# Keys, values and bias of the second attention: made in a stage of their own, or in the first stage and kept in DRAM

## The reference, cut to what matters

```
hd = DIM // HEADS            # 16
scale = hd ** (-0.5)
q = (x @ Wq).reshape(B, N, HEADS, hd)
k = (context @ Wk).reshape(B, M, HEADS, hd)
v = (context @ Wv).reshape(B, M, HEADS, hd)
scores = q k^T * scale, masked by context_mask; softmax over the 77 rows; times v; then @ Wo
```

## Time and profile before

| | us |
|---|---|
| median of 3 runs (lowest, highest) | 1813.8 (1812.35, 1814.16) |
| the profiled execution, its own time | 1812.47 |
| span of the profiled execution | 1810.7 |
| PE busy | 1554.4 (86%) |
| DVE busy | 1110.4 (61%) |
| ACT busy | 824.6 (46%) |
| POOL busy | 706.7 (39%) |

### The profile page before, as it was taken

The page is one execution under the profiler, slowest core; times in us unless marked ns, Lnnn a source line. Parts: engine busy times, 40 slices in busy tenths (PEclk is TensorE's granted clock), DMA queues, the critical chain, the costliest instruction groups (busy, mean ns, idle before and its releaser), DMA issues. The chain is left out here.

```text
span 1810.7 us, 39194 instructions
## 1 busy us (share of the span) xinstructions
PE 1554.4 (86%) x12604; PEld 1143.3 (63%) x12605; DVE 1110.4 (61%) x1945; ACT 824.6 (46%) x1516; POOL 706.7 (39%) x521
## 2 busy tenths in 40 slices
PE   4798798897977599999999994899978599999996
PEld 1433334234337478888888881777768478888885
DVE  4687787787868634444554441888868744444443
ACT  1563654645633355555554440566754322222221
POOL 2401303104000125555554431677760045556554
PEclk9899899898985799999999995799995799999998
DMA  4321311322228245555542222200006243333333
GB/s 134 111 71 47 123 62 46 116 69 97 67 89 279 90 148 139 139 139 139 136 116 46 45 34 52 70 25 24 25 1 233 86 134 61 58 58 59 60 59 44
DMA packets 104311, 159.85 MB, mean 88 GB/s; under 512 B 10810, under 2 KB 69998, under 8 KB 104110
## 3 DMA queue, kind: packets, MB, share of 16 engines
q1 hardware_dynamic: 73007, 117.52, 19.9%
q0 software_dynamic: 29952, 40.91, 12.9%
q10 hardware_dynamic: 1279, 0.46, 0.1%
HBM read 91.49 MB, written 67.37 MB: 88 GB/s over the span
## 5 line engine op out<-in xcount | busy, mean ns | idle before, releaser
L1243 PE MATMUL e_ph<-e_zTt,weights_a 128*128 128x256 f16 x3744 | 426.7, 275 | 29.9 <-issue 27.5
L1243 PEld LDWEIGHTS e_ph<-e_zTt,weights_a 128*128 x3744 | 361.6, 98 | 94.6 <-issue 50.4
L1376 DVE TENSOR_TENSOR e_hl<-e_h,e_hh 128x512 f16<-128x512 f32 x156 | 104.5, 690 | 230.7 <-ACT e_hh L1342 230.7
L1197 POOL DMA_INDIRECT e_zt<-token_parts,slot_token x156 | 163.4, 1048 | 210.6 <-issue 198.8
L1328 ACT ACTIVATE e_h<-e_ph,e_b 128x256 f32<-128x256 f32 x312 | 130.6, 470 | 234.9 <-PE e_ph L1243 157.5
L1207 POOL DMA_INDIRECT token_rows<-e_ysb,slot_token x78 | 148.2, 1900 | 208.9 <-DVE e_ysb L1393 194.7
L1257 PE MATMUL e_pyt<-weights_b,e_hh 128*128 x1248 | 210.7, 273 | 0.7 <-DVE e_ysb L1393 0.7
L640 ACT ACTIVATE probs<-lower_banks,shift 128x1024 f32<-128x1024 f32 x128 | 137.5, 1110 | 92.1 <-PE lower_banks L500 91.7
L1207 POOL DMA_INDIRECT out_dram<-e_ysb,slot_token x78 | 124.4, 1595 | 131.0 <-DVE e_ysb L1397 107.4
L1257 PE MATMUL e_pyt<-weights_b,e_hl 128*128 x624 | 170.1, 273 | 0.0
L1367 DVE SCALAR_TENSOR_TENSOR e_g<-e_ph,e_h 128x512 f32<-128x512 f32 x78 | 53.9, 691 | 173.8 <-PE e_ph L1243 173.8
(11 more groups left out here) (228 smaller groups left out, 2847.0 us busy)
## 6 DMA issues: line engine op xcount, KB each, us to landing
weight_parts<-w_split SPq DMA_DIRECT2D x32, 512.0 KB, 3.3
weights_a<-weight_parts SPq DMA_DIRECT2D x16, 1024.0 KB, 7.5
x_sb<-in_u SPq DMA_DIRECT2D x24, 512.0 KB, 5.1
weight_parts<-x_sb SPq DMA_DIRECT2D x24, 512.0 KB, 3.4
w_raw<-in_w1T SPq DMA_DIRECT2D x16, 512.0 KB, 4.4
w_raw<-in_w2T SPq DMA_DIRECT2D x16, 512.0 KB, 4.7
weights_b<-weight_parts SPq DMA_DIRECT2D x8, 1024.0 KB, 9.5
token_parts<-x_sb SPq DMA_DIRECT2D x8, 1024.0 KB, 5.3
```

Source lines behind the costliest of these rows:

```text
L1197: pool.indirect_dma_start(zt[:, i % 2, c, :], None, g.zrows, at).then_inc(ld[i % 2], 16)
L1243: last = pe.matmul(ph[:, q, f, :], up_w(wp, e, k, 2 * q + f), zTs[:, s, 2 * zp + k, :], start=(n == 0), stop=(n == 5))
L1376: dve.tensor_tensor(hl[:, s, 2 * q:2 * q + 2, :], src[:, q % 2], hh[:, s, 2 * q:2 * q + 2, :], ALU.subtract).then_inc(lo_done, 1)
```

## The change: what it does, and the diff

The first stage gets what the context stage did. ACT issues the loads of Wv, Wk and the mask behind its nine loads; PE makes the values and keys behind the eight `kv` products, in the banks of `tr`; ACT spreads the values behind its copy of `vctx`; DVE converts the mask behind `summarise` and makes the keys last; POOL's zeros and head masks stand behind its constants. The results `g.k1`, `g.v1`, `g.bias1` are stored to DRAM at the start of the first attention's SP stream, behind the three stores of zeros. `attention1_context` is gone. At the start of `attention1` ACT issues the loads of Wq, keys, bias, values and Wo, and waits stand where each is first used.

```diff
--- before
+++ after
@@ line 173 @@
             act.dma_start(gk[:], a["kn_g"].partition_broadcast(P)).then_inc(ld_g, 16)
+            for w, src in ((wv1, a["Wv1"]), (wk1, a["Wk1"])):
+                act.dma_start(w[:, 0, :], src[0:P, :]).then_inc(ld_second, 16)
+                act.dma_start(w[0:DC - P, 1, :], src[P:DC, :]).then_inc(ld_second, 16)
+            act.dma_start(mask8[:], a["mask1"].partition_broadcast(P)).then_inc(ld_second, 16)
@@ line 188 @@
             act.copy(g.vctx[:], kv[:, :, D:2 * D]).then_inc(sq_done, 1)
+            act.wait_ge(v1_mm, 1)
+            act.wait_ge(made, 1)
+            for b in range(B):
+                own_v = tr[0:M, b // 2, b % 2 * D:b % 2 * D + D].rearrange("p (h o d) -> p h o d", o=2, d=HD1)
+                for o in range(2):
+                    act.copy(g.v1[:, b, o:H1:2, o * HD1:(o + 1) * HD1], own_v[:, :, o, :]).then_inc(v1_ev, 1)
             act.wait_ge(v_step, 16)
@@ line 209 @@
             pool.wait_ge(g.consts, 4)
+            pool.memset(g.v1[:], 0.0).then_inc(made, 1)
+            pool.affine_select(out=own2[:], in_=g.ones[:, 0:8], compare_op=ALU.is_ge, fill=0.0, base=0,
+                               pattern=[[-HD1, 8]], channel_multiplier=1).then_inc(made, 1)
+            pool.wait_ge(made, 2)
+            pool.affine_select(out=own[:], in_=own2[:], compare_op=ALU.is_ge, fill=0.0, base=HD1 - 1,
+                               pattern=[[HD1, 8]], channel_multiplier=-1).then_inc(made, 1)
             pool.wait_ge(v_step, 9)
@@ line 248 @@
             summarise(dve, g, 1, 0, T, True)
+            dve.wait_ge(ld_second, 16 * 5)
+            dve.tensor_copy(mask1[:], mask8[:]).then_inc(k1_step, 1)
+            dve.wait_ge(made, 3)
+            dve.tensor_reduce(odd[:], own[:].rearrange("p (r o) -> p o r", o=2), AX.X, ALU.add).then_inc(k1_step, 1)
+            dve.wait_ge(k1_step, 2)
+            dve.tensor_scalar(g.bias1[:], mask1[:], 1.0, -MASKED, ALU.subtract, ALU.mult).then_inc(k1_step, 1)
             dve.wait_ge(p_step, 4)
@@ line 268 @@
             dve.tensor_tensor(khl[:, 1], kn[:], khl[:, 0], ALU.subtract).then_inc(v_step, 1)
+            dve.wait_ge(k1_mm, 1)
+            for hg in range(2):
+                dve.scalar_tensor_tensor(kT1[:, hg].rearrange("p b m -> p (b m)"), tr[:, 2 + hg, 0:B * M], SCALE1,
+                                         mask1[:].rearrange("p b m -> p (b m)"), ALU.mult, ALU.mult).then_inc(k1_step, 1)
+            dve.wait_ge(k1_step, 5)
+            for b in range(B):
+                for hg in range(2):
+                    dve.tensor_tensor(g.k1[:, b, hg], kT1[:, hg, b:b + 1, :].to_broadcast([P, 2, M]),
+                                      odd[:].rearrange("p (o n) -> p o n", n=1).to_broadcast([P, 2, M]),
+                                      ALU.mult).then_inc(k1_done, 1)
+            dve.wait_ge(k1_done, 2 * B)
             dve.wait_ge(v_step, 22)
@@ line 291 @@
             last.then_inc(kv_done, 1)
+
+            pe.wait_ge(ld_second, 16 * 5)
+            for b in range(B):
+                for k, r in ((0, P), (1, DC - P)):
+                    last = pe.matmul(tr[0:M, b // 2, b % 2 * D:b % 2 * D + D], g.ctxT[0:r, k, b, 0:M], wv1[0:r, k, :],
+                                     start=(k == 0), stop=(k == 1))
+            last.then_inc(v1_mm, 1)
+            for hg in range(2):
+                for k, r in ((0, P), (1, DC - P)):
+                    last = pe.matmul(tr[:, 2 + hg, 0:B * M], wk1[0:r, k, hg * P:(hg + 1) * P], g.ctxT[0:r, k, :, 0:M],
+                                     start=(k == 0), stop=(k == 1))
+            last.then_inc(k1_mm, 1)
+            pe.wait_ge(v1_ev, 2 * B)
             pe.wait_ge(hi_done, 1)
@@ line 393 @@
                          ).then_inc(g.cleared, 16)
+            for home, made in zip(g.second, (g.k1, g.v1, g.bias1)):
+                sp.dma_start(home, made[:]).then_inc(second_kept, 16)
             for i, gate in enumerate((a["routerT"], a["gate"])):
@@ line 422 @@
             sp.wait_ge(g.cleared, 48)
+            sp.wait_ge(second_kept, 48)
             for i in range(2):
@@ line 1430 @@
-def attention1_context(nc, g, a, at):
...
-def attention1(nc, g, at):
+def attention1(nc, g, a, at):
@@ line 1613 @@
                     t = base + c
+                    if c == 0:
+                        pe.wait_ge(ld_q, 16)
                     pe.wait_ge(zT_ev, t + 1)
@@ line 1648 @@
                 if live(d):
+                    if d == 0:
+                        pe.wait_ge(ld_o, 16)
                     pe.wait_ge(o_ev, base + d + 1)
@@ line 1657 @@
         def _(act):
+            act.dma_start(at.wq[:], a["Wq1"].rearrange("(k p) n -> p k n", p=P)).then_inc(ld_q, 16)
+            act.dma_start(at.k[:], g.second[0]).then_inc(ld_k, 16)
+            act.dma_start(at.bias[:], g.second[2]).then_inc(ld_k, 16)
+            act.dma_start(at.v[:], g.second[1]).then_inc(ld_v, 16)
+            act.dma_start(at.wo[:], a["Wo1"].rearrange("(k p) n -> p k n", p=P)).then_inc(ld_o, 16)
+
             def body(base, b0, c, live):
                         act.wait_ge(s_done, base + c)
+                    else:
+                        act.wait_ge(ld_k, 32)
                     act.copy(keys[:].rearrange("p (n h) o m -> p n h o m", n=1),
@@ line 1681 @@
                 if live(d + 1) and (d + 1) % TB == 0:
+                    if d + 1 == 0:
+                        act.wait_ge(ld_v, 16)
                     act.copy(v[:].rearrange("p (o h) d -> p o h d", o=1), at.v[:, bass.ds(b0 + (d + 1) // TB, 1)]
@@ line 1750 @@
                         dve.wait_ge(pt_done, 4 * (t - SLOT) + 4)
+                    if c == 1:
+                        dve.wait_ge(ld_k, 32)
                     dve.wait_ge(s_done, t + 1)
@@ line 1827 @@
+    g.second = [nc.dram_tensor(f"second_{n}", shape, F32, kind="Internal").ap()
+                for n, shape in (("k", [P, B, 2, 2, M]), ("v", [M, B, H1, 32]), ("bias", [P, B, M]))]
+
     def rows_of(w, k0, k):
@@ line 1840 @@
             m = Mem(nc, st)
+            g.k1 = m.sb("k1_made", [P, B, 2, 2, M])
+            g.v1 = m.sb("v1_made", [M, B, H1, 32])
+            g.bias1 = m.sb("bias1_made", [P, B, M])
             g.kctx = m.sb("kctx", [P, 2, 2 * B, MP], F16)
@@ line 1871 @@
             at.wo = m.sb("wo1", [P, 2, D])
-            attention1_context(nc, g, a, at)
-            attention1(nc, g, at)
+            attention1(nc, g, a, at)
```

More of the change, by code:

```diff
@@ L136, in attention0_inputs @@
         gabs = m.sb("gabs", [P, 1])
+        wk1 = m.sb("wk1", [P, 2, D])
+        wv1 = m.sb("wv1", [P, 2, D])
+        mask8 = m.sb("mask8", [P, B, M], U8)
+        mask1 = m.sb("mask1f", [P, B, M])
+        own = m.sb("own", [P, 8])
+        own2 = m.sb("own2", [P, 8])
+        odd = m.sb("odd", [P, 2])
+        kT1 = m.sb("kT1", [P, 2, B, M])
         kv = m.ps("kv_c", [M, B, 2 * D])
@@ L144, in attention0_inputs @@
         hi_done, kt_done, kt_ev = m.sem("c_hi"), m.sem("c_ktd"), m.sem("c_ktev")
+        ld_second, made, v1_mm, k1_mm = m.sem("k_ld"), m.sem("k_made"), m.sem("k_vmm"), m.sem("k_kmm")
+        v1_ev, k1_step, k1_done = m.sem("k_vev"), m.sem("k_step"), m.sem("k_bd")
         recycle(nc, g, m)
@@ L385, in attention0 @@
         w_hi, w_lo = m.sem("a_w_hi"), m.sem("a_w_lo")
+        second_kept = m.sem("a_second")
         recycle(nc, g, m)
@@ L1560, in attention1 @@
         ld = [m.sem(f"b_ld{i}") for i in range(2)]
+        ld_q, ld_k, ld_v, ld_o = (m.sem("b_ld_" + n) for n in "qkvo")
         recycle(nc, g, m)
```

74 lines of the change are left out of this document (removed).

## The result

| | changed kernel | kernel before, same chip |
|---|---|---|
| median (lowest, highest), us | 1791.0 (1786.71, 1792.0) | 1813.14 |
| ratio, 95% interval | 0.9874 [0.986, 0.9888] | |
| the profiled execution, and its span | 1786.71, 1785.0 | 1812.47, 1810.7 |

1791.0 was measured where 1792 was forecast; the change makes the kernel 1.3% faster. The same kernel, run three times more on other occasions, gave 1792.37, 1793.99 and 1789.46.

The account below looks back on a forecast made before the run. PE, busy 86% of the span, was taken to set the time almost everywhere, but the context stage stood alone. Terms -24.14 + 1.5 + 0.4 + 0.8 = -21.4 us against 1812.5 gave 1791.0, as a median 1792; range 1788 to 1798.

Parts of the forecast that it names:

- Context stage: Between the experts and the second attention: loads, products, copies and block change all go, -24.14 us.
- First stage: Kernel's start: added loads delay x, DVE makes keys last, so the stage ends 1.5 us later; bounds +0.8 and +4.
- First attention: Its start: three more stores delay the first weight fetch by 5.6 us, hidden in 19 us before first use: 0.
- Second attention's entry: Its start: x's first tile +0.4 us from sharing with Wq; ACT's wait for keys and bias +0.8.
- The clock: Second attention: PE's grant rises at the same time after the stage's own start, 0, with 1.5 us either way.
- A: Second attention's entry paid in full: keys +4, x 0.75, first stage +3.5, giving 1798 us; chance 0.10.
- B: More than forecast: first stage hides its DVE work, PE starts the first attention warm, giving 1789 us; chance 0.09.
- C: Second attention, tiles after the fifth: PE's clock stays at half, +5.4 us a tile, slower than before; chance 0.03.
- D: Context stage's place: something else held it, such as x's load waiting for scattered rows; gain shrinks to 1810 us; chance 0.04.

Follow-up runs that it names:

- first_only: Changed kernel with the context stage and second attention of before put back, first stage still making and storing keys, values, bias; 1812.32 us, ratio 0.9984 to the kernel before.
- ordered: Changed kernel with Wk, Wv and mask loads moved behind x on SP's queue, and values and Wo loaded later in the second attention; 1788.85 us, ratio 0.9858.
- stores4: Changed kernel with the three stores of the first attention made four times, each behind the landing of the one before; 1801.92 us, ratio 0.9929.
- before2: The kernel before, word for word, against itself; 1815.33 against 1815.42 us, ratio 1.0.
- pe_pad: The kernel before with 24 unread PE passes, shaped like the values' and keys', added behind the `kv` products; 1816.62 us, ratio 1.0005.
- delay1: The kernel before with 1 us added: POOL clears an unused tile behind its roots in the first stage; 1815.7 us, ratio 1.0005.
- entry_only: Changed kernel without the first stage's making of keys, values and bias: zeros are stored, and the second attention loads them; 1790.02 us, ratio 0.9867 to the kernel before.
- warm_more: Changed kernel with 12 extra PE products at the second attention's start and 21 more in PE's pauses of its first steps; 1790.71 us, ratio 0.9851.

## Why the prediction was right

**Context stage, -24.14.** Held within 0.04 us: from the last scatter's issue to the second attention's start it is 30.78 us before and 6.68 after, 24.10 less. It could be read off because nothing lay beside the stage. That the engine busy times hardly changed shows that the same work is now done under cover.

**First stage, forecast +1.5, measured +0.99 (1.01 in `first_only`).** The way there was right. x landed at 25.39, 1.23 later, where 1.24 was worked out from bytes over 350 GB/s; 0.16 of it is a later issue and 1.07 a longer landing. The reason of the 1.07 is open, since with the weights behind x in `ordered` only 0.3 of it came back. PE's part came as forecast, by the lengths of the earlier trace rows: values and keys took 8.59 and 5.36 us and ended at 42.25 (42.8 in the sum), only 0.3 ahead of DVE's use of them; in `ordered` DVE waited 0.75 for them. DVE ended at 45.37 instead of 45.95, and this is the term that was too large. The roots on POOL took 5.46 instead of 6.50, a full microsecond that no row had promised; they were not on the path, since DVE ended later.

**First attention, 0.** ACT's L672 ran without idle at 68.23. The fetch itself went out at 52.66, 5.0 later, more than three stores' issues: two gate-row issues behind them lasted 1.39 and 1.49 us where 0.51 and 0.69 stood before. `stores4` shows that the cover was real, and that some 10 us more of it were left; by the forecast's rows it was 9 (19 less 4.4 and 5.6).

**Second attention's entry, forecast +0.4 and +0.8, measured about +0.1 beside the trace of before.** x's first tile landed 2.64 after its issue. The +0.4 was taken on top of the 3.6 of before, but that 3.6 is no constant: `first_only`, whose context stage stands as before, shows 2.12, and `before2`, the same kernel as before, 2.00 (in `pe_pad` it was 1.97, in `delay1` 3.89).

```profile
1120.47 0.83 SPq L1640 DMA_DIRECT2D x_sb<-token_rows  x2
1122.59 0.43 DVE L1803 BATCH_NORM_STATS2 stats<-x_sb 128x6 f32<-128x256 f32 x1 [2.60 <-DMA x_sb<-token_rows]
```

```profile
1121.62 0.84 SPq L1580 DMA_DIRECT2D x_sb<-token_rows  x2
1123.61 0.43 DVE L1743 BATCH_NORM_STATS2 stats<-x_sb 128x6 f32<-128x256 f32 x1 [2.48 <-DMA x_sb<-token_rows]
```

So what the entry costs depends on the trace that it is set beside. The product with Wq begins 6.71 us after the start in the changed kernel, 7.01 in before and 5.52 in `before2`; the second tile's score add 16.23, 16.13 and 14.65; the fifth's 34.43, 34.85 and 33.88. That the +0.1 is so small is luck of the trace read; beside the fast landing the entry costs 1.2 at the first product, as much as was forecast, and about 0.5 at the fifth tile.

Whether x and Wq share the DMA engines, as the prediction took, can't be read here. Keys and bias had landed at 5.85 after the start, not 7.3. Part of this is that the DMA engines moved more than the 350 GB/s of the forecast, part that the 3.2 us beyond the bytes were taken from the slow landing of before (x's tile took 2.64 here, 2.3 beyond its bytes). The changed kernel's row of GB/s, 40 slices of 1090 to 1112 us, has

```profile
GB/s 35 30 136 73 0 0 0 0 0 0 0 26 192 283 341 443 430 385 395 406 296 300 250 179 201 240 116 6 26 210 110 130 9 207 82 194 4 190 101 183
```

The issue-to-landing times are 4.7 us for the keys and 4.8 for the bias. The wait did move to ACT's keys copy as foreseen (23.59 idle, released by the bias) and `zT` started 0.07 us behind the end of the turn, where it was 0.03 in before. By what the Trainium skill states in "DMA: Bandwidth & Descriptors", section "Latency and other measured facts", that HBM's access time goes from 0.2 us on average to 2 us at high load, they were to be up to 1.8 later still. These rows show no such rise: the landing was 1.45 earlier than the estimate without it. What nobody foresaw is the third tile, 9.24 after the start behind values and Wo instead of 5.84. It filled a slack: in `ordered`, with that tile 3.2 us sooner, the fifth tile's score add came no more than 0.1 sooner.

**The clock, 0.** The grant rose 32.2 us after the second attention's own start in before (1152.4) and 31.2 after it in the changed kernel (1126.7); over all traces without added products it lies between 30.9 and 34.2. So it follows the stage's start, as taken, and its moment moved by 1.0 us in this pair, within the 1.5 either way. Windows of the changed kernel, to be set beside the last two of the earlier trace rows:

```profile
1120.00:1126.00 6.00, 4.53 (x29) 3.65 (x30) 5.86 (x10) 3.40 (x6) 4.82 (x3) 0.50 0.32 92
1126.00:1130.00 4.00, 4.00 (x65) 3.40 (x64) 3.18 (x7) 2.60 (x6) 3.86 (x3) 0.91 0.39 112
1145.00:1175.00 30.00, 28.22 (x377) 23.54 (x378) 26.65 (x49) 20.68 (x40) 22.16 (x15) 1.00 0.01 2
```

**What the sum did not have.** About 2 us in the experts of layer 0, 600 us behind the last edit, where with the first half a pause of 2.08 us is one of 1.8 and the clock isn't lowered. It is shown that this comes with the whole first half (`first_only` has it, `entry_only` and the kernel before lack it), that neither PE's products alone, nor a first stage one microsecond longer, nor the stores bring it, and that the pause is longer by 0.29 us that ACT loses ahead of it. ACT's stream holds the eight value copies more in just the nine traces with the short pause, and DVE's the keys and the bias; a kernel with the one or the other alone was not tried, and the cause stays open. From the first attention's first store to the end of layer 0's experts are 1051.2 to 1053.7 us in the five traces without the first half and 1048.5 to 1051.1 in those with it (without `stores4`), so the pair in the table, at -1.56, shows less of it than most.

The change's own terms as measured make -24.1 + 1.0 + 0.1 = -23.0, and the experts' 2 us would make it -25; the four comparisons of medians gave -22.1, -22.9, -20.6 and -26.0. What holds the middle of them above -25 was not found for certain; an entry that costs up to a microsecond more than 0.1, and the half clock at the end of the second attention, different from execution to execution, are of that size. So the mechanism held, the stage's 24.1 us and what stays of them, but that the number came within 1 us is in part luck: the terms were 1.6 too high together, one of 2 us was lacking, and the measured kernel's own medians lie 4.5 us apart.

**The rivals.** A, the entry paid in full, fell: of the 8.3 us that it put on keys, x and first stage together, 1.1 were measured. B, more than forecast, came nearer to the true terms, but not by its reasons: DVE's work was not hidden, and the first projections of the first attention took 3.73 us for four, no less than the 3.42 before. C, the clock staying at half, fell with the 31.2 us. D fell with the 24.10.

## What to carry to other kernels

A stage that stands alone between two barriers is worth its whole length, start to start, and what replaces it is worth only what exceeds the idle time already there: look for the engine that is last in the new place, and for the first instruction that waits for the new loads. Here a pause of TensorE of 2.08 us in place of 1.8, 600 us behind the last edit, went with 1.67 us of slower products: before a gain of 0.2% is put down to the edit, compare the granted clock in stretches that the edit doesn't touch, and follow a pause back through the engines that end it, since "issue" as its releaser says nothing. A landing time read once (3.6 us for a tile) is no constant: two traces of one and the same kernel had 3.61 and 2.00, so it needs a range of its own, and a small term should be compared with more than one trace of before.

## What the runs showed of the hardware

```profile
29.00:36.00 7.00, 7.00 (x15) 2.18 (x14) 6.96 (x21) 1.39 (x2) 2.91 (x1) 1.00 0.00 0
36.00:44.00 8.00, 7.45 (x26) 3.19 (x26) 7.49 (x26) 2.46 (x9) 5.40 (x1) 1.00 0.00 1
```

```profile
47.97 3.73 PE L532 MATMUL lower_banks<-wqkv,lnT 128*128 128x512 f32 x4 [0.47 <-ACT lnT L646]
...
52.40 1.88 PE L532 MATMUL lower_banks<-wqkv,lnT 128*128 128x512 f32 x4
```

- A busy PE at half clock is not raised for being busy alone: 15.04 of 18 us in `warm_more`, 7.00 of 7 in the context stage.
- GpSimd's power of 128x32 took 6.50 us in before, before2, delay1, pe_pad and entry_only, and 5.46 in every kernel with the whole first half. What makes the difference is open.
- The issue of one and the same DMA has no fixed length. The two loads of Wk took 1.58 and 0.97 us on ACT behind eleven other issues, and 0.36 and 0.53 first on SP in the context stage of before; the two gate-row loads went from 0.51 and 0.69 to 1.39 and 1.49 with three more stores ahead of them.
